# First layer's attention: the max with zero moved from VectorE to GpSimd, with VectorE's square widened from 1056 to 1664 columns

## What is computed

```
sq = q2 + swapaxes(k2) - 2.0 * einsum('bhqd,bhkd->bhqk', Q, K)
dist = sqrt(maximum(sq, 0.0))
W = (SHEP_EPS + dist) ** (-2)
W = W / (SHEP_EPS + sum(W, axis=-1))
A = einsum('bhqk,bhkd->bhqd', W, V)
```

## Time and profile before

| | us |
|---|---|
| median of 3 runs | 7601.04 |
| lowest and highest run | 7600.39 to 7608.52 |
| the profiled execution | 7607.89 |
| its span in the profile | 7605.8 |
| busy in the span: VectorE, ScalarE | 7175.8, 6931.5 |
| busy in the span: TensorE matmuls, GpSimd | 4245.9, 2209.8 |
| mean granted TensorE clock | 0.701 of full speed |

### The profile page before, as it was taken

One profiled execution on the slowest core, in us unless ns is written; L12 is line 12 of the kernel. 1 busy time (PEld: TensorE's weight loads), 2 busy tenths in 40 slices (PEclk: granted clock), 3 DMA queues, 4 the chain that ended last, 5 costly groups with the idle time before them and its releaser, 6 DMA issues. The chain is left out here.

```text
span 7605.8 us, 60658 instructions
## 1 busy us (share of the span) xinstructions
PE 4245.9 (56%) x17232; PEld 1292.8 (17%) x17232; DVE 7175.8 (94%) x6927; ACT 6931.5 (91%) x4385; POOL 2209.8 (29%) x1348
## 2 busy tenths in 40 slices
PE   6666666676766667444444454444444444544545
PEld 3221212121222233111111111111111111111112
DVE  7899999999999966999999999999999999999996
ACT  3799999999999934999999999999999999999995
POOL 0000000000000000454544445454544545454452
PEclk9888888888888878666566665656666665665667
DMA  3100000000000022000000000000000000000002
GB/s 128 43 18 11 16 12 16 12 16 12 16 12 14 10 102 102 6 11 7 6 11 6 6 11 6 6 11 6 6 11 6 10 6 6 10 6 6 10 2 69
DMA packets 113675, 148.41 MB, mean 20 GB/s; under 512 B 17038, under 2 KB 98857, under 8 KB 112634
## 3 DMA queue, kind: packets, MB, share of 16 engines
q1 hardware_dynamic: 104314, 138.54, 5.8%
q10 hardware_dynamic: 9216, 8.39, 0.3%
HBM read 91.55 MB, written 55.31 MB: 19 GB/s over the span
## 5 line engine op out<-in xcount | busy, mean ns | idle before, releaser
L741 PE MATMUL psS<-q_stack,k_stack 102*128 102x512 bf16 (+1 forms) x4096 | 1795.1, 534 | 2464.6 <-DVE work L1058 1617.3
L715 POOL TENSOR_TENSOR work<-work 128x1024 f32<-128x1024 f32 x1024 | 1915.4, 1907 | 10.2
L764 PE MATMUL psO<-work,v_tile 128*32 128x512 f32 x8192 | 1432.5, 822 | 732.0 <-DVE work L1073 727.5
L933 DVE SCALAR_TENSOR_TENSOR work<-work,psS 128x1024 f32<-128x1024 f32 x1024 | 1240.2, 1211 | 42.4 <-ACT work L891 41.9
L1049 DVE TENSOR_SCALAR work<-psS 128x1024 f32<-128x1024 f32 x1024 | 1206.7, 1218 | 71.0 <-issue 41.2
L1058 DVE TENSOR_TENSOR work<-psS,work 128x1024 f32<-128x1024 f32 x1024 | 1199.8, 1213 | 0.0
L1089 DVE SCALAR_TENSOR_TENSOR work<-work 128x2048 f32<-128x2048 f32 x512 | 1138.5, 2285 | 58.3 <-ACT work L1011 56.7
L891 ACT ACTIVATE work<-psS 128x1024 f32<-128x1024 f32 x1024 | 1099.6, 1074 | 70.6 <-PE psS L741 45.4
L1006 ACT ACTIVATE work<-work 128x4096 f32<-128x4096 f32 x256 | 921.2, 3612 | 126.9 <-DVE work L1058 117.1
L906 ACT ACTIVATE work<-work 128x2048 f32<-128x2048 f32 x512 | 1005.3, 1964 | 0.4 <-ACT ffn_out L823 0.4
L741 PEld LDWEIGHTS psS<-q_stack,k_stack 102*128 102x128 bf16 (+1 forms) x4096 | 257.5, 105 | 4136.7 <-DVE work L1058 2509.8
(11 more groups left out here) (126 smaller groups left out, 3444.8 us busy)
## 6 DMA issues: line engine op xcount, KB each, us to landing
qk_parts<-work SPq DMA_DIRECT2D x64, 384.0 KB, 3.2
q_stack<-qk_parts SPq DMA_DIRECT2D x384, 64.0 KB, 2.2
k_stack<-qk_parts SPq DMA_DIRECT2D x384, 64.0 KB, 2.2
ffn_in<-xT_store SPq DMA_DIRECT2D x64, 128.0 KB, 2.5
y_store<-ffn_out ACTq DMA_DIRECT2D x64, 128.0 KB, 1.7
work<-y_store SPq DMA_DIRECT2D x8, 1024.0 KB, 12.0
work<-in_x SPq DMA_DIRECT2D x1, 4096.0 KB, 14.4
xn_store<-work SPq DMA_DIRECT2D x1, 4096.0 KB, 13.0
```

The lines of the kernel that those rows point to most:

```text
L715: nc.gpsimd.tensor_tensor(part, part, part, ALU.mult).then_inc(s_pp, 1)
L741: last = nc.tensor.matmul(m.psS[half][:, q * 512:(q + 1) * 512], m.k_stack[b][0:rows, kt * P:(kt + 1) * P], m.q_stack[b][0:rows, c:c + 512 ...
L764: last = nc.tensor.matmul(m.psO[b][VW * q:VW * (q + 1), :], m.v_tile[b][:, kt, :], ring[:, u % RING, q * 512:(q + 1) * 512], start=kt == 0 ...
L933: nc.vector.scalar_tensor_tensor(part, part, 0.5 / SHEP_EPS, m.psS[half][:, :], ALU.add, ALU.mult).then_inc(s_y, 1)
```

## The change

GpSimd gets a step of its own for every unit, `guard`: it clamps the whole slot to between zero and the largest fp32 number. It waits until both quotients of its unit are done (s_y) and until VectorE's square of the unit three before it is done (s_wd), which in VectorE's list is the square that stands between the two quotients of the next unit. VectorE's list becomes quotient of half 0, square, quotient of half 1. All lags behind it grow by one unit, and ScalarE's share of the square falls from 992 to 384 columns, so VectorE's grows from 1056 to 1664. GpSimd's copy into v_tile moves from the head's start to its places 3 and 19.

```
+F32_MAX = 3.4028234663852886e38
...
-    LAG_PV = 5
-    LAG_INV, LAG_SQ = 2, 3
+    LAG_PV = 6
+    LAG_INV, LAG_SQ = 3, 4
...
-    ACT_SQ = 992
+    ACT_SQ = 384
...
+            def guard(c):
+                pool.wait_ge(s_y, 2 * c + 2)
+                if c + 1 >= LAG_SQ:
+                    pool.wait_ge(s_wd, c + 2 - LAG_SQ)
+                slot = ring[:, c % RING, :]
+                nc.gpsimd.tensor_scalar(slot, slot, F32_MAX, 0.0, ALU.min, ALU.max).then_inc(s_m, 1)
+
             def head(h, first, last):
                 if L == 0:
-                    for b in range(B):
-                        value_tile(h, b, first)
+                    for u in range(UNITS):
+                        if u % KT == 3:
+                            value_tile(h, u // KT, first)
+                        guard(UNITS * h + u)
...
                         if u < UNITS:
                             quotient(u, 0)
-                        if u <= UNITS and not (first and u < 1):
-                            dve.wait_ge(s_y, 2 * c)
-                            slot = ring[:, (u - 1) % RING, :]
-
-                            nc.vector.tensor_scalar(slot, slot, 0.0, None, ALU.max).then_inc(s_m, 1)
-                        if u < UNITS:
-                            quotient(u, 1)
                         if not (first and u < LAG_SQ):
                             dve.wait_ge(s_v, c - LAG_SQ + 1)
                             part = ring[:, (u - LAG_SQ) % RING, ACT_SQ:T]
                             nc.vector.tensor_tensor(part, part, part, ALU.mult).then_inc(s_wd, 1)
+                        if u < UNITS:
+                            quotient(u, 1)
```

## The result

| | before | after |
|---|---|---|
| median of the runs, us | 7600.89 | 7414.58 |
| lowest to highest | 7600.39 to 7608.52 | 7411.12 to 7425.23 |
| the profiled execution | 7607.89 | 7411.12 |

The forecast was 7442 us, in a range of 7385 to 7530, so the sign and the mechanism held and the gain came out some 27 us larger.

The account below looks back on a forecast made before the run. VectorE and ScalarE were taken as full together, GpSimd as empty. 4.35 + 0.07 + 0.06 = 4.48 us a unit against 4.80, over 512 units, with +5, gave -159 us: 7442 us, range 7385 to 7530.

Parts of the forecast that it names:

- VectorE's list: VectorE per unit: two quotients at 1.13 us and the widened square at 1.80, 4.06 us; 4.22 with small steps.
- The guard: GpSimd's clamp of 2048 columns takes 2.0 us, starts 0.09 us after VectorE's square, and is done before the next.
- Rival C: GpSimd's clamp is slower, 3.78 us; the loop square, guard, square paces from 2.91; about 8051 us; chance 0.06.
- Who holds whom: VectorE operations with two SBUF operands take turns with GpSimd's; PSUM quotients are not held; squares of hidden lose 0.9 us.
- rival B: Nothing meets the guard: squares of hidden slip in, waits vanish, 4.25 us a unit, about 7324 us; chance 0.05.
- rival D: The guard also holds VectorE's quotients: 6.1 us a unit, about 8272 us; chance 0.02.
- The small prices: On VectorE the tile's end loses some tenths, GpSimd's v_tile copy meets a square: together +0.02 us a unit.
- The waits: VectorE's idle time per unit: 0.07 us as before, plus 0.06 for unevenly spaced quotients and TensorE's lower clock.
- rival A: TensorE paces the changed stage, needing 4.55 us a unit at its low clock: 4.67 a unit, about 7539 us; chance 0.15.
- The drain: At the phase's end the values product comes one unit later and a guard replaces a max: +5 us, once.

Follow-up runs that it names:

- experiment 2: Changed kernel with ScalarE's share of the square left at 992 columns, so only the max moves to GpSimd: 7564.6 us, ratio to before 0.9954.
- experiment 3: Kernel before the change with only ScalarE's share of the square cut from 992 to 384 columns: 7892.1 us, ratio to before 1.0382.
- experiment 5: Changed kernel with GpSimd's guard followed by a second clamp of the slot's first 512 columns: 7555.9 us, ratio to before 0.9940.
- experiment 6: Changed kernel with the guard as one operation, max with 0.0, in place of min and max: 8149.5 us, ratio to before 1.0723.
- experiment 1: Changed kernel with the guard waiting only for its unit's quotients, not for VectorE's square: 7706.2 us, ratio to before 1.0137.
- Experiment 11: Changed kernel with the squares of hidden ahead of the big square and ScalarE's feed-forward store issued in the next unit: 7346.3 us, ratio to before 0.9663.

## Why the prediction was right, point by point

- **VectorE's list.** Predicted 4.06 us a unit, measured 4.06 (1558.60 to 1562.66). Loss of the max and growth of the square came as priced; experiments 2 and 3 show that either alone is worth little or less than nothing, as two engines busy 98.6% and 97.4% of the stretch before would lead one to expect.
- **The guard.** Predicted 2.0 us from the second layer's row at 1045 ns, measured 1.89. It starts 0.15 us after the square, not 0.09. The row was a good guide by luck of form: it was times and plus, one of the two pairs found fast. From "one input, two operations" the time does not follow, as the 7.08 us of the max pair shows. The estimate of 1.76 us that the prediction sets beside its sum, for bodies of at most two operations and before any fixed part, fits the two fast pairs and not the 5.36 of one operation. Rival C had 0.06. Its loop is borne out where the form is a fast one: for the 2.59 us of experiment 5 it gives 1.80 + 0.09 + 2.59 = 4.48, measured 4.49. For the slow form of experiment 6 it is not.
- **Who holds whom.** This came as forecast: the quotient with a PSUM operand 1216 ns beside the guard, the squares held until GpSimd's end in experiments 1 and 5, those of `hidden` +0.86 us each (1.46 from start to start in place of 0.60). So rivals B and D are out; D's price, which holds every VectorE operation, goes beyond the words that the prediction cites for it. The Trainium skill states it (SBUF — State Buffer, Who interferes with whom): a VectorE instruction with at most one SBUF input, outside the faster modes that use two ports, does not contend with GpSimd, and one with two contends with a GpSimd instruction that reads SBUF. The trace agrees, for the guard's form: 1216 ns against 1211, and 1.54 us against 0.68.
- **The small prices.** I gave the tile's end and the copy into v_tile 0.02 us a unit; they cost none (425 ns, and 451 for the copy against 400).
- **The waits.** This is the term that was mis-sized: 0.07 + 0.06, measured 4.41 - 4.06 - (2 x 1.46 + 1.40) / 16 = 0.08. The added 0.06 for TensorE at the lower level (rival A in small) came on ScalarE, whose waits for scores grew from 34.8 us in 2300 to 71.3 in 2150, but hardly on VectorE, whose idle time before the quotients was 32.4 us and had been 25.0. The clock rose, to 0.87. Experiment 11 shows that about half of VectorE's idle time came from ScalarE waiting for its copy before the store: it stood at place 0 of the tile, 14.7 of 29.6 us from 500 to 2400, and went when the store was moved. With the small prices the mis-sizing is 0.07 x 512 = 36 us, against 38 between the forecast for the profiled execution, 7449, and its 7411. That they meet is in part luck: the phase gained 189.4 us where 159 were forecast, 30 more, and the other 7 fell outside it.
- **The drain.** From the last quotient's end to ScalarE's copy of psO it is 12.2 us, was 7.6: +4.6, against +5.

One thing the prediction left out did no harm here, but would mislead elsewhere. It tells by the count of SBUF operands whom GpSimd holds. In the second layer of the kernel before, a VectorE operation with a single SBUF operand is held as well. Its line, then one of them on VectorE:

```profile
L1069 DVE TENSOR_SCALAR work<-work x256: 378/804/2080, 3070.9 to 7498.5; 128x448 f32<-128x448 f32 x128
...
3487.88 2.08 DVE L1069 TENSOR_SCALAR work<-work 128x448 f32<-128x448 f32 x1
```

GpSimd beside it:

```profile
3487.67 2.04 POOL L715 TENSOR_TENSOR work<-work 128x1024 f32<-128x1024 f32 x1
```

The 43 of them that start with GpSimd idle take 378 to 385 ns; the 195 that start beside its line 715 take 423 to 2080. This one ends at 3489.96, 0.25 us behind GpSimd. Undisturbed they are also faster than a square of as many columns (610 ns). So the count of operands is not enough: the quotient, whose other operand is in PSUM, is free, as the earlier trace rows shows of its kind, and a VectorE tensor_scalar from SBUF to SBUF could not be put in its place.

What stays open is the rest of the waits, 11.6 us in 1900, and why ScalarE waits for scores as long with half of the feed-forward work.

## What to carry to other kernels

When two engines are both full, look for the third and move work through both: the piece that one can give up to the empty engine, and the split between the two full ones, in the same edit. In these traces work on GpSimd was free beside VectorE's operations that had one operand in PSUM, and not beside those with two in SBUF, nor beside a tensor_scalar from SBUF to SBUF. So release it at the end of the last one that it would hold, count what is left of that window (here 0.13 us), and give its consumer one more unit of lag. Before giving GpSimd a tensor_scalar, measure that very pair of operations.

## What the runs showed of the hardware that I had not expected

A GpSimd tensor_scalar over 128 x 2048 fp32 costs 1.89 us with min and max, 1.90 with multiply and add, 5.36 with one operation alone, and 7.08 with max and max or multiply and max. Adding an operation made it 2.8 times as fast.

Beside the slow form VectorE is let go before the pass ends. Timelines of VectorE, then of GpSimd in experiment 6:

```profile
1499.06 3.27 DVE L964 TENSOR_TENSOR hidden<-hidden 128x512 f32<-128x512 f32 x1
...
1507.46 3.35 DVE L955 TENSOR_TENSOR work<-work 128x1664 f32<-128x1664 f32 x1
```

```profile
1498.17 5.36 POOL L723 TENSOR_SCALAR work<-work 128x2048 f32<-128x2048 f32 x1 [0.17 <-DVE work L955]
1505.43 5.36 POOL L723 TENSOR_SCALAR work<-work 128x2048 f32<-128x2048 f32 x1 [1.91 <-DVE work L955]
```

The square of `hidden` ends at 1502.33, 4.2 us after the start of GpSimd's pass, which runs on to 1503.53. The wide square ends 5.4 us after the start of its pass. Beside the fast form the same two end 0.54 and 1.74 us behind GpSimd, so these are what they need once they are let go. Taken off, both were let go 3.6 us after the start of the slow pass, some 1.7 before its end, and ran at their own rate from there. The other held ones from 500 to 2400 us fit: 40 squares of `hidden` start 0.75 or 0.90 us after the pass and all end 4.17 to 4.18 after its start, and 265 wide squares end 5.37 to 5.38 after it. So VectorE was held first and free then, and not slowed throughout, and this is why squares and passes overlap in experiment 6. Why the last 1.7 us of the slow pass hold nobody is not shown.
